# Six sequences' last factor and final addition, issued by GpSimd instead of VectorE

## The reference, cut to what matters

```python
def block(h, p):
    r = _retention(h, wk)                      # causal, weighted by q.k
    a, gate = jnp.split(r @ w1 + b1, 2, axis=-1)
    m = _groupnorm1(a * silu(gate) @ w2 + b2, gg, gb)
    y = m + h
    f = gelu(y @ wf1 + bf1_) @ wf2 + bf2_
    return _layernorm(f + y, lg, lb)
...
xn = _layernorm(x, axis=-1)
x = x + layers(xn) + experts(xn)
```

## Time and profile before

| what | us |
|---|---|
| median of 3 runs | 463.49 |
| lowest and highest | 463.42, 464.23 |
| the profiled execution, its own time | 466.27 |
| the profiled execution, its span | 464.4 |

### The profile page before, as it was taken

The page is one execution under the profiler, slowest core; times in us unless marked ns, Lnnn a source line. Parts: engine busy times, 40 slices in busy tenths (PEclk is TensorE's granted clock), DMA queues, the critical chain, the costliest instruction groups (busy, mean ns, idle before and its releaser), DMA issues.

```text
span 464.4 us, 7880 instructions
## 1 busy us (share of the span) xinstructions
PE 443.1 (95%) x2302; PEld 320.2 (69%) x2302; DVE 385.3 (83%) x1347; ACT 220.4 (47%) x411; POOL 162.5 (35%) x198
## 2 busy tenths in 40 slices
PE   3999989999999999999999999999999999999982
PEld 2788867777777777777777777777777777765440
DVE  3879889989888887988788777877888887999996
ACT  2124365554545445555554454555555545545331
POOL 1433102535443433533233323433233332334542
PEclk9989999999999999999999999999999999999996
DMA  8900000000000000000000000000000000000103
GB/s 234 250 2 0 2 2 0 2 0 1 1 1 2 1 0 1 2 0 1 1 1 0 2 0 1 1 2 1 2 1 0 2 0 2 1 1 7 39 29 108
DMA packets 13497, 8.20 MB, mean 18 GB/s; under 512 B 608, under 2 KB 13456, under 8 KB 13456
## 3 DMA queue, kind: packets, MB, share of 16 engines
q1 hardware_dynamic: 13376, 7.68, 5.9%
q10 hardware_dynamic: 80, 0.02, 0.0%
HBM read 5.60 MB, written 2.10 MB: 17 GB/s over the span
## 4 chain that ended last, share of the span: by engine, by line
PE 87%; DVE 7%; issue 2%; DMA 1%; ACT 1%; DVEq 0%; SPq 0%
PE pair L406 6%; PE bank L325 6%; PE pair L331 6%; PE bank L308 6%; PE bank L381 6%; PE bank L254 6%; PE bank L399 6%; PE bank L417 5%; PE bank L413 5%; PE bank L315 5%; PE pair L333 5%; PE bank L250 4%; PE bank L246 4%; PE bank L247 4%; PE bank L357 3%
## 5 line engine op out<-in xcount | busy, mean ns | idle before, releaser
L1125 POOL TENSOR_TENSOR gn_r<-gn_v,minus_half 128x1 f32<-128x1 f32 x32 | 17.6, 550 | 174.0 <-DVE gn_v L907 174.0
L1135 POOL TENSOR_TENSOR sum_four<-prod 128x512 f32<-128x512 f32 x32 | 40.5, 1266 | 74.5 <-DVE prod L967 74.5
L615 ACT ACTIVATE a_in<-bank,params 128x512 f32<-128x512 f32 x32 | 22.0, 688 | 84.6 <-PE bank L250 84.6
L647 ACT ACTIVATE va<-bank,ln_off,ln_r 128x128 f32<-128x128 f32 x128 | 48.5, 466 | 17.8 <-DVE ln_off L959 17.8
L331 PEld LDWEIGHTS pair<-va,scores 128*128 128x128 f32 x256 | 43.5, 193 | 18.9 <-issue 16.3
L967 DVE TENSOR_TENSOR prod<-bank,route 128x512 f32<-128x512 f32 x64 | 43.8, 684 | 8.6 <-PE bank L250 8.5
L331 PE MATMUL pair<-va,scores 128*128 128x129 f32 x256 | 49.8, 278 | 1.1 <-issue 1.1
L246 PE MATMUL bank<-expert_w,xn 128*128 128x512 f32 x64 | 42.3, 661 | 1.5 <-DVE zt L936 1.5
L325 PEld LDWEIGHTS bank<-gt,vt 128*128 128x128 f32 x256 | 33.6, 192 | 14.2 <-issue 13.1
L1130 POOL TENSOR_TENSOR ln_r<-ln_v,minus_half 128x4 f32<-128x4 f32 x32 | 32.8, 1024 | 14.3 <-DVE ln_v L951 13.2
L333 PE MATMUL pair<-past,gt 128*128 128x129 f32 x192 | 37.3, 276 | 0.0
(11 more groups left out here) (159 smaller groups left out, 1100.4 us busy)
## 6 DMA issues: line engine op xcount, KB each, us to landing
x_in<-in_L_attn_x_dram SPq DMA_DIRECT2D x8, 256.0 KB, 5.3
out_dram<-x_in SPq DMA_DIRECT2D x8, 256.0 KB, 2.3
wf<-in_L_attn_Wf_dram SPq DMA_DIRECT2D x2, 512.0 KB, 6.4
kqv<-in_L_attn_Wkqv_dram SPq DMA_DIRECT2D x1, 576.0 KB, 6.2
expert_rows<-in_L_ffn_We_dram SPq DMA_DIRECT2D x1, 512.0 KB, 8.3
wm<-in_L_attn_Wm_dram SPq DMA_DIRECT2D x1, 384.0 KB, 6.6
wm<-in_L_attn_Wm_dram SPq DMA_DIRECT2D x1, 256.0 KB, 4.9
expert_b<-in_L_ffn_be_dram SPq DMA_DIRECT2D x16, 4.0 KB
```

The costliest lines, as they stand in the source:

```text
L647: last = act.activation(va[:, n % NB, c, 0:D], Z_BANK[:, c * P:(c + 1) * P], ACT.Identity, bias=ln_off[:, i, c:c + 1], scale=ln_r[:, i, c: ...
```

## The change

For the first six sequences of the last layer (items 24 to 29) `scale_last` and `add_result` are issued by POOL. For items 30 and 31 they stay on DVE. The semaphores tg_set and result_set are split in two, one for each engine, and SP waits for the one or the other. The arithmetic, its tiles and the wait conditions of the two steps are the same.

```diff
+    ON_POOL = 6
...
             for k in range(NB):
-                sp.wait_ge(result_set, k + 1)
+                sp.wait_ge(*((result_pool, k + 1) if k < ON_POOL else (result_dve, k - ON_POOL + 1)))
...
             def slot(n):                                   # DVE
-                step(scale_last, n - 12, LAST)
+                step(scale_last, n - 12, LAST + ON_POOL)
...
-                step(add_result, n - 14, LAST)
+                step(add_result, n - 14, LAST + ON_POOL)
...
+            def scale_last(n):                             # POOL
+                k = n % NB
+                pool.wait_ge(v_set, n + 1)
+                pool.tensor_tensor(va[:, k, :, 0:D], va[:, k, :, 0:D], last_g, ALU.mult).then_inc(tg_pool, 1)
+
+            def add_result(n):
+                k = n % NB
+                pool.wait_ge(tg_pool, k + 1)
+                pool.wait_ge(v_taken, n + 1)
+                pool.tensor_tensor(x_in[:, k], va[:, k, :, 0:D], x_in[:, k], ALU.add).then_inc(result_pool, 1)
...
             def slot(n):                                   # POOL
                 if n == 17:
                     rest_of_xn(5)
+                step(scale_last, n - 14, LAST, LAST + ON_POOL)
                 step(sum_to_two, n - 14)
                 if n == 3:
                     round_xn(1)
                 step(group_factor, n - 11)
                 step(sum_to_one, n - 14)
+                step(add_result, n - 15, LAST, LAST + ON_POOL)
```

More of the change, by code:

```diff
@@ L179, in retention_moe @@
             "experts_a experts_b prod_a prod_b four_set two_set one_set x_added")
-        bias_done, tg_set, result_set = several("bias_done tg_set result_set")
+        bias_done, tg_pool, tg_dve, result_pool, result_dve = several("bias_done tg_pool tg_dve result_pool result_dve")
+        last_g = ln_bc[:, 0, :].unsqueeze(1).to_broadcast((P, C, D))
         def step(op, n, first=0, end=ITEMS):
@@ L990, in scale_last @@
             def scale_last(n):
-                if n == LAST:
-                    dve.wait_ge(bc_in, 32)
+                k = n % NB
                 dve.wait_ge(v_set, n + 1)
-                dve.tensor_tensor(va[:, n % NB, :, 0:D], va[:, n % NB, :, 0:D],
-                                  ln_bc[:, 0, :].unsqueeze(1).to_broadcast((P, C, D)), ALU.mult).then_inc(tg_set, 1)
+                dve.tensor_tensor(va[:, k, :, 0:D], va[:, k, :, 0:D], last_g, ALU.mult).then_inc(tg_dve, 1)
             def add_result(n):
                 k = n % NB
-                dve.wait_ge(tg_set, k + 1)
+                dve.wait_ge(tg_dve, k - ON_POOL + 1)
                 dve.wait_ge(v_taken, n + 1)
-                dve.tensor_tensor(x_in[:, k], va[:, k, :, 0:D], x_in[:, k], ALU.add).then_inc(result_set, 1)
+                dve.tensor_tensor(x_in[:, k], va[:, k, :, 0:D], x_in[:, k], ALU.add).then_inc(result_dve, 1)
             dve.memset(minus_half[:, :], -0.5)
@@ L1130, in norm_factor @@
                 pool.tensor_tensor(ln_r[:, n % 2, :], ln_v[:, n % 2, :], minus_half[:, :], ALU.pow).then_inc(ln_rstd, 1)
+            def scale_last(n):
[3 more added lines that the diff above has]
+            def add_result(n):
+                k = n % NB
+                pool.wait_ge(tg_pool, k + 1)
+                pool.wait_ge(v_taken, n + 1)
+                pool.tensor_tensor(x_in[:, k], va[:, k, :, 0:D], x_in[:, k], ALU.add).then_inc(result_pool, 1)
             def sum_to_four(n):
```

## The result

| kernel | median us | runs | lowest and highest |
|---|---|---|---|
| before | 463.86 | 6 | 463.42, 466.10 |
| changed | 480.88 | 6 | 480.57, 482.28 |

The ratio is 1.0347, with a 95% interval of 1.0313 to 1.0382. The change makes the kernel 17.0 us slower; 16.4 were forecast, and 479.9 us.

What follows compares the result with a forecast made beforehand. PE bounds until about 420 us, then DVE; turns and end 35.85 + 8.6 + 9.9 + 6.0 against 45.84, plus 0.9 entry, make 15.4; with 1.0 for the clock, 16.4 on 463.49: 479.9 us, range 475 to 483.5.

Steps and rivals of the forecast that it cites:

- The loop: Waits through DVE, ACT and POOL, gone round once per slot: 11.95 us, against slots of 9.55 and 9.61 before.
- The three turns: From ln_mr 26 to ln_mr 29, each turn at 11.95 us, together 35.85.
- The entry: Into ln_mr 26, first turns absorbed while PE is the bound: it starts at 416.3 to 416.4, +0.9 us.
- The turn from 29 to 30: ln_mr 29 to 30, no group norm left, so DVE's slot plus POOL's tail: 8.6 us.
- the clock: PE at half clock after idling in the last two turns: 1.0 us more taken, bounds 0 and 2.0 for both.
- The turn from 30 to 31: ln_mr 30 to 31, sum_two holding up ln_mr and DVE's own factor ahead of the addition: 9.9 us.
- The end: From ln_mr 31 to DVE's end: 6.0 us, against 6.60 before, with one moved addition of 0.60 gone.
- Lock only: Rival: DVE and POOL excluding each other on reads is the whole cost, POOL's waits covered; 464.1 us, chance 0.04.
- Faster: Rival: POOL's additions fit into its gaps and nine times 0.60 us come off DVE; 458.1 us, chance 0.04.
- The looser loop: Rival: some link is off the path, up to some 3 us less in three turns; 471 to 475, chance 0.08.
- The colder PE: Rival: PE's clock at half from the third turn on; 480.9 up to 484 us, chance 0.04 beyond 483.
- The rule on reads: Two-input VectorE instructions and GpSimd instructions reading SBUF exclude each other for the whole instruction; a tiny gn_s took 1.18 us.

Runs made afterwards that it cites:

- the best version: Kernel before with only five of the sixteen instructions on GpSimd, placed where it idles in its last three slots: 464.56 us against 465.36, ratio 0.9981.

## Why the prediction was right, step by step

**The loop** was right, in its members, its order and its length: 12.25 and 12.16 for 11.95. What the prediction didn't say is that the addition's wait is enough to close one: without the factors the turns were still 11.06 and 11.28, and without the additions ln_r came on time up to item 29. The three turns come to 36.01 where the sum had 35.85, closer than the single turns, and that is in part luck. The two moved instructions are a little shorter: 1.18 instead of the 1.27 of the earlier trace rows, and the next starts 1.14 after them, where I had taken 1.22. And ln_r is longer: 1.47 in the first two turns instead of 1.02, beside a y of 1.84 on DVE instead of 0.74. I had let ln_r pass without being held up by what reads beside it. So the first two turns are 0.2 to 0.3 longer than the sum, and the third, 11.60, is 0.35 shorter. There I had y stand ahead of the addition and make up for the missing mixed. It stands behind add_biases, and it only holds the addition up:

```profile
446.11 1.55 POOL L1142 TENSOR_TENSOR x_in<-va,x_in 128x512 f32<-128x512 f32 x1 [3.03 <-DVE x_in L991]
```

That is 1.55 for 1.18, 0.37 us where mixed had taken some 0.5, and ln_r is back at 1.03.

**The entry** was +0.9 and came out at 0.70 (12.06 - 11.36). Its wording, that all starts until 415 us stay within 0.5 of those before, was not right: DVE waits 1.07 and 1.46 us for gn_r in the two slots ahead, and everything behind gn_s is late by that much. It is made good only at the border of the slots, where DVE had idled and where a factor is gone.

**The turn from 29 to 30** had 8.6 and at most 1.0 for the clock. It was 10.07, and 8.57 once PE was kept at its upper level. So the sum without the clock was exact. The clock was undersized, 1.5 for 1.0, in one trace each. I had counted zt's product and its turning. But the product of the biases on PE, 2.07 instead of 1.12, also holds up add_biases, by 0.49.

**The turn from 30 to 31** had 9.9 and was 9.63, with the clock back at full. DVE's own factor held the addition up by 0.31 (1.49 for 1.18) where I had taken 0.47. **The end** had 6.0 and was 6.00. In all 16.57 for 16.4. The mechanism was right; that the total is this close is luck in part, since the clock's and the first turns' excess and the savings of the third turn, the last turn and the entry nearly cancel.

**The rivals.** Lock only (464.1) is out by the kernel whose moved instructions don't read. Faster (458.1) had one condition, that add_biases ends 3.5 us ahead of the next ln_mr. It does not, and where the queue was changed so that it needn't, ten of the 17 us were gone. The looser loop did not occur. The colder PE did, in one turn of this kernel and in three of the one with the additions alone, and it was the main reason why that one missed its forecast.

**What was wrong without mattering.** DVE's busy time fell by 3.9 us (385.3 to 381.4), not by 7 to 8. An instruction that is held up by the other engine's reads counts as busy: the two long y alone make up for 2.2 us. POOL's rose by 13.6, not 15.

**Which term was sized badly in an experiment**: the factors alone. I had given gn_r's delay, and nothing for what the factor pushes along behind it on POOL (sum_four into ln_v). The rule on reads had been applied to the large instructions only.

## What to carry to other kernels

Before moving an instruction to a less busy engine, read what stands behind it in that engine's queue and who waits for that: the busy share says whether there is room, the queue says whether there is a loop. Add the loop up, link by link; if it is longer than the period of the engine that is the bound, it sets the time. And an instruction that hides a wait is worth nothing when it goes: look what is late next.

## What the runs showed of the hardware that I had not expected

- One-element and four-element instructions are held up for the whole of a 128x512 one on the other engine: gn_c 1.13 us for 0.21, ln_v 1.14 for 0.17, ln_mr 1.15 for 0.15. ln_v has a single input.
- It also goes the other way: POOL's ln_r, a power of four elements, took 1.47 for 1.02 beside DVE's y.
- The length of a gap on PE doesn't by itself give the clock level behind it. In the changed kernel the products behind a gap of 2.52 us ran at the lower level at once (0.63). With 1.88 us of added products and a gap of 0.81 us the upper level was held. Ahead of the next product lay a gap of 4.28 us: the first three matmuls behind it still ran at the upper level (0.39), and those from 463.54 us on at the lower.
- The clock that is granted between 20 and 30 us varies from run to run (1.00, 0.83 and 0.66 in twelve traces) and moves the whole kernel by about 2 us between the first two and by 4 to 5 between the first and the last, more than the gain of the best version.
